# A new order table for every engine of a two-layer AdaLN kernel, all instructions unchanged

## What is computed

```python
mod = (_silu(L0_c) @ L0_wmod).reshape(L0_c.shape[0], 6, 1, -1)
h = _layernorm(x, axis=-1) * (1 + ca) + sa
x = x + ga * _L0_attn_ref(h, L0_attn_w_qkv, L0_attn_w_out)
h = _layernorm(x, axis=-1) * (1 + cb) + sb
x = x + gb * _L0_ffn_ref(h, L0_ffn_gate_kernel, ...)
...
h = _layernorm(x, axis=-1) * (1 + ca) + sa
x = x + ga * _L1_attn_ref(h, ...)
h = _layernorm(x, axis=-1) * (1 + cb) + sb
x = x + gb * _L1_ffn_ref(h, ...)
```

## Time and profile before

| | us |
|---|---|
| median of 3 runs | 1070.87 |
| the runs | 1074.27, 1070.87, 1070.3 |
| span of the profiled execution | 1072.8 |
| TensorE busy | 916.9 (85%) |
| VectorE busy | 773.2 (72%) |
| ScalarE busy | 656.1 (61%) |
| GpSimd busy | 428.5 (40%) |
| mean granted TensorE clock | 0.941 |

### The profile page before, as it was taken

How to read it: one execution, slowest core, us unless ns; L and a number is a source line. 1 busy time by engine, 2 the same in 40 slices (tenths; PEclk the granted TensorE clock), 3 DMA queues, 4 the chain that set the end, 5 groups by cost and what they waited for, 6 DMA issues and landing times. The chain is left out here.

```text
span 1072.8 us, 15618 instructions
## 1 busy us (share of the span) xinstructions
PE 916.9 (85%) x5176; PEld 507.8 (47%) x5176; DVE 773.2 (72%) x1467; ACT 656.1 (61%) x1176; POOL 428.5 (40%) x537
## 2 busy tenths in 40 slices
PE   4147778998899899999998899999998899879876
PEld 2111134443454355654444655455565365558744
DVE  6565678768866877788768686888878766447675
ACT  2235564666666768667667576776856756755442
POOL 3241042325131826554324265662545525265310
PEclk9557899999999999999999999999999899979978
DMA  8510214001300040115000014032010010010001
GB/s 233 163 55 30 63 39 101 31 2 56 60 1 2 14 118 9 40 31 126 4 1 14 22 45 99 31 90 41 18 35 19 3 38 2 9 41 7 18 10 35
DMA packets 54536, 47.09 MB, mean 44 GB/s; under 512 B 12393, under 2 KB 50025, under 8 KB 53114
## 3 DMA queue, kind: packets, MB, share of 16 engines
q1 hardware_dynamic: 53898, 45.85, 16.8%
q10 hardware_dynamic: 560, 0.26, 0.1%
HBM read 30.97 MB, written 14.73 MB: 43 GB/s over the span
## 5 line engine op out<-in xcount | busy, mean ns | idle before, releaser
L1565 DVE TENSOR_REDUCE negmax<-scores_for_max 128x2 f32<-128x1024 f32 x252 | 307.6, 1221 | 67.9 <-PE scores_for_max L940 66.0
L1277 ACT ACTIVATE probs<-scores 128x1024 f32<-128x1024 f32 x256 | 262.4, 1025 | 114.9 <-PE scores L964 112.2
L974 PE MATMUL weighted_values<-probs,vaug 128*32 128x512 f32 x1024 | 143.2, 634 | 3.6 <-ACT probs L1277 3.6
L1038 PEld LDWEIGHTS shared_ab<-eo,mu 128*128 128x128 f32 x1024 | 128.6, 191 | 35.6 <-issue 25.2
L1038 PE MATMUL shared_ab<-eo,mu 128*128 128x128 f32 x1024 | 141.1, 281 | 3.7 <-ACT scaled L1391 2.0
L1963 POOL TENSOR_TENSOR acc<-acc,scaled 128x512 f32<-128x512 f32 x55 | 71.7, 1304 | 169.6 <-ACT scaled L1391 169.6
L572 PE MATMUL expert_units<-hb_hi,e_lo 128*128 128x512 f32 x224 | 111.9, 500 | 16.7 <-DVE mu L1706 9.8
L940 PE MATMUL scores_for_max<-ks,qs 48*128 48x512 bf16 x504 | 102.1, 402 | 26.5 <-DVE negmax L1565 22.3
L1700 DVE SCALAR_TENSOR_TENSOR mu<-th,expert_units 128x512 f32<-128x512 f32 x112 | 76.7, 685 | 66.1 <-ACT th L1319 65.6
L964 PE MATMUL scores<-qs,ks 51*128 51x512 bf16 x512 | 102.2, 396 | 25.4 <-ACT probs L1277 23.7
L1319 ACT ACTIVATE th<-expert_units 128x512 f32<-128x512 f32 x112 | 66.9, 597 | 83.0 <-PE expert_units L574 81.8
(11 more groups left out here) (320 smaller groups left out, 1591.5 us busy)
## 6 DMA issues: line engine op xcount, KB each, us to landing
parts_d<-parts SPq DMA_DIRECT2D x15, 384.0 KB, 2.5
qs<-parts_d SPq DMA_DIRECT2D x14, 384.0 KB, 6.1
ks<-parts_d SPq DMA_DIRECT2D x14, 384.0 KB, 9.3
w<-in_L_ffn_w SPq DMA_DIRECT2D x16, 256.0 KB, 3.8
parts_d<-parts SPq DMA_DIRECT2D x15, 256.0 KB, 2.7
xp<-in_L_attn_x SPq DMA_DIRECT2D x8, 256.0 KB, 2.9
probs<-in_L_ffn_w_kernel SPq DMA_DIRECT2D x2, 1024.0 KB, 7.9
x<-in_L_attn_x SPq DMA_DIRECT2D x8, 256.0 KB, 2.9
```

What stands on the lines that cost most here:

```text
L974: last = nc.tensor.matmul(pv[32 * j:32 * j + 32, :], vaug[:, kt, PAIRS * (j // 2) + GP * g + j % 2, :], probs[:, kt % 2, j % 2, j // 2, :] ...
L1038: last = nc.tensor.matmul(m0[:, at], mu[:, (2 * e + f) % 4, at], eo[:, e, f, :], start=(f == 0), stop=(f == HALVES - 1))
L1277: nc.scalar.activation(probs[:, kt % 2, j, :, :].rearrange("p m s -> p (m s)"), se[:, :], ACT.Exp)\
L1565: V.tensor_reduce(negmax[:, g % 2, :, n], max_bank(b, g, n)[:, :].rearrange("p (m s) -> p m s", m=2), AX, ALU.max, negate=True)\
```

## The change

Only `SLOTS` differs. All 1344 TensorE, 872 ScalarE, 1032 VectorE, 272 GpSimd and 136 SyncE entries are there before and after; 1271, 816, 954, 252 and 123 of them stand at another place in their engine's order. The lines of the diff that name the steps of the text below, cut from the whole table:

```diff
@@ -67,237 +67,239 @@
 SLOTS = {
-    ("P", "load"): dict(sp=(1, 19, 28, 31, 48, 57, 79, 84)),
...
-    ("P", "xT"): dict(pe=(30, 60, 72, 178, 324, 531, 662, 880)),
...
-    ("P", "v"): dict(pe=(54, 62, 77, 199, 328, 645, 668, 1017), act=(14, 47, 106, 195, 274, 397, 465, 632)),
...
-    ("P", "stack"): dict(sp=(27, 40, 50, 61, 69, 83, 99, 108)),
...
-    ("C", "xT"): dict(pe=(465, 559, 807, 938, 1060, 1169, 1260, 1324)),
...
-    ("C", "out"): dict(pe=(538, 647, 885, 1012, 1117, 1227, 1307, 1335)),
...
-    ("C", "xT3"): dict(pe=(564, 768, 899, 1024, 1133, 1239, 1317, 1338)),
...
-    ("P", "e0hi"): dict(act=(20, 21, 24, 27, 38, 45, 46, 50)),
-    ("P", "e1hi"): dict(act=(49, 58, 59, 60, 85, 95, 100, 146)),
-    ("P", "whhi"): dict(act=(25, 28, 29, 33, 34, 43, 44, 102)),
...
-    ("P", "mod1"): dict(dve=(123, 194, 218, 222, 240, 244, 264, 298)),
...
-    ("P", "e0lo"): dict(dve=(176, 177, 180, 186, 193, 196, 197, 223)),
...
-    ("P", "raw"): dict(sp=(2, 3, 5, 11, 13, 16, 17, 18)),
...
+        ("P", "xT"): dict(pe=(54, 65, 69, 197, 327, 492, 644, 811)),
+        ("P", "v"): dict(pe=(62, 66, 172, 312, 471, 618, 778, 936), act=(51, 58, 110, 192, 289, 381, 482, 586)),
...
+        ("C", "xT"): dict(pe=(344, 512, 678, 854, 1003, 1134, 1260, 1324)),
...
+        ("C", "out"): dict(pe=(449, 638, 814, 976, 1097, 1205, 1302, 1337)),
+        ("C", "xT3"): dict(pe=(463, 657, 827, 994, 1104, 1219, 1312, 1338)),
...
+        ("P", "e0hi"): dict(act=(2, 15, 16, 17, 18, 19, 41, 42)),
+        ("P", "e1hi"): dict(act=(3, 43, 44, 45, 46, 47, 48, 49)),
...
+        ("P", "whhi"): dict(act=(6, 20, 21, 22, 23, 24, 27, 28)),
...
+        ("P", "e0lo"): dict(dve=(85, 86, 87, 88, 89, 90, 91, 92)),
...
+        ("P", "mod1"): dict(dve=(150, 157, 160, 161, 162, 163, 164, 165)),
...
+        ("P", "raw"): dict(sp=(1, 4, 5, 7, 8, 9, 10, 11)),
+        ("P", "load"): dict(sp=(2, 19, 34, 47, 55, 67, 79, 92)),
...
+        ("P", "stack"): dict(sp=(35, 39, 45, 54, 65, 78, 94, 104)),
```

More of the change, by code:

```diff
@@ L83 @@
[L83 to L88, removed]
@@ L160 @@
-    ("A", "wog"): dict(dve=(255, 339, 420, 534, 602, 731, 792, 924)),
-    ("B", "load"): dict(sp=(21, 55, 65, 77, 89, 103, 118, 128)),
-    ("B", "oT"): dict(pe=(169, 323, 477, 633, 786, 944, 1108, 1256)),
-    ("B", "ot"): dict(act=(109, 198, 283, 390, 480, 590, 693, 797)),
-    ("B", "y"): dict(pe=(170, 326, 479, 636, 793, 951, 1112, 1257)),
-    ("B", "x1"): dict(dve=(268, 356, 438, 540, 631, 733, 841, 936)),
-    ("B", "stats"): dict(dve=(269, 357, 440, 541, 633, 734, 842, 937)),
-    ("B", "rstd"): dict(pool=(37, 68, 89, 127, 152, 190, 217, 247)),
@@ L294 @@
-    ("P", "wT"): dict(pe=(26, 27, 28, 32, 33, 35, 39, 53)),
-    ("P", "wsplit"): dict(dve=(84, 85, 93, 101, 102, 104, 107, 110)),
-    ("P", "colm"): dict(pe=(31, 34, 36, 37, 42, 43, 44, 45, 46, 48, 49, 50, 51, 52, 57, 286)),
-    ("P", "cols"): dict(dve=(87, 112, 118, 119, 120, 121, 122, 191, 192, 199, 201, 202, 204, 211, 242, 281)),
-    ("P", "modpe"): dict(pe=(40, 47, 55, 56, 242, 335, 368, 414)),
-    ("P", "raw"): dict(sp=(2, 3, 5, 11, 13, 16, 17, 18)),
-    ("P", "late"): dict(sp=(4, 22, 23, 26, 32, 34, 35, 42)),
+        ("C", "out0"): dict(pe=(1, 2, 3, 4, 5, 6, 7, 1329)),
@@ new lines @@
+        ("C", "upb"): dict(pe=(8, 9, 10, 11, 12, 13, 14, 15, 16, 17, 18, 19, 20, 21, 1334, 1336)),
+        ("C", "row"): dict(pe=(22, 23, 24, 25, 26, 27, 28, 1254)),
+        ("P", "wT"): dict(pe=(29, 30, 31, 32, 33, 34, 35, 36)),
+        ("P", "colm"): dict(pe=(37, 38, 39, 40, 41, 42, 43, 44, 45, 46, 47, 48, 49, 50, 51, 52)),
+        ("P", "modpe"): dict(pe=(53, 55, 56, 57, 58, 59, 60, 61)),
+        ("P", "xT"): dict(pe=(54, 65, 69, 197, 327, 492, 644, 811)),
+        ("P", "v"): dict(pe=(62, 66, 172, 312, 471, 618, 778, 936), act=(51, 58, 110, 192, 289, 381, 482, 586)),
@@ new lines @@
+        ("P", "proj"): dict(pe=(63, 64, 67, 68, 73, 85, 204, 219, 333, 364, 529, 556, 707, 763, 818, 839)),
+        ("A", "max"): dict(pe=(70, 71, 72, 74, 75, 76, 77, 78, 79, 81, 82, 83, 86, 90, 92, 95, 97, 101, 103, 105, 108,
[11 rows of a table added]
+        1214), dve=(221, 222, 223, 225, 226, 227, 228, 229, 230, 231, 232, 233, 235, 236, 237, 238, 239, 240, 241,
[11 rows of a table added]
+        ("A", "mT"): dict(pe=(80, 100, 120, 142, 167, 194, 236, 265, 317, 337, 373, 418, 461, 491, 521, 555, 627, 647,
+        674, 715, 774, 808, 838, 877, 922, 965, 999, 1036, 1105, 1133, 1182, 1224)),
@@ new lines @@
+        ("P", "silu"): dict(act=(4, 5, 25, 26, 29, 30, 31, 32, 33, 34, 35, 36, 37, 38, 39, 40), dve=(102, 103, 112,
+        113, 114, 115, 116, 117, 118, 119, 120, 121, 122, 123, 124, 125)),
+        ("P", "whhi"): dict(act=(6, 20, 21, 22, 23, 24, 27, 28)),
+        ("P", "small"): dict(act=(7, 8, 9, 10, 11, 12, 13, 14)),
+        ("P", "hT"): dict(act=(50, 57, 62, 126, 200, 304, 397, 504)),
+        ("P", "split"): dict(act=(52, 55, 59, 63, 67, 77, 135, 144, 210, 230, 337, 351, 443, 481, 517, 534), dve=(167,
@@ new lines @@
+        ("P", "stats"): dict(dve=(93, 168, 219, 275, 349, 442, 536, 639)),
+        ("P", "wsplit"): dict(dve=(94, 95, 96, 97, 98, 99, 100, 101)),
+        ("P", "whlo"): dict(dve=(104, 105, 106, 107, 108, 109, 110, 111)),
+        ("P", "cols"): dict(dve=(126, 127, 136, 137, 138, 139, 140, 141, 142, 143, 144, 145, 146, 147, 148, 149)),
+        ("P", "mod1"): dict(dve=(150, 157, 160, 161, 162, 163, 164, 165)),
+        ("P", "lo"): dict(dve=(151, 152, 153, 154, 155, 156, 158, 159), pool=(2, 20, 26, 45, 68, 102, 134, 163)),
@@ new lines @@
+        ("P", "rot"): dict(dve=(166, 171, 218, 220, 224, 234, 293, 300, 359, 378, 484, 495, 588, 619, 657, 673)),
+        ("A", "wog"): dict(dve=(170, 274, 357, 453, 553, 655, 754, 848)),
+        ("P", "split3"): dict(dve=(172, 203, 204, 205, 206, 207, 208, 209, 210, 211, 212, 213, 214, 215, 216, 217),
+        pool=(8, 9, 24, 29, 32, 36, 48, 53, 76, 81, 111, 115, 144, 156, 172, 178)),
+        ("A", "onorm"): dict(dve=(243, 253, 261, 269, 291, 311, 329, 344, 372, 395, 415, 435, 465, 482, 503, 525, 556,
@@ new lines @@
+        ("C", "rstd3"): dict(pool=(89, 130, 165, 197, 215, 235, 262, 272)),
+        ("P", "raw"): dict(sp=(1, 4, 5, 7, 8, 9, 10, 11)),
+        ("P", "load"): dict(sp=(2, 19, 34, 47, 55, 67, 79, 92)),
+        ("P", "late"): dict(sp=(3, 6, 12, 13, 14, 15, 16, 17)),
+        ("P", "modst"): dict(sp=(18, 20, 21, 22, 23, 24, 25, 26)),
+        ("B", "load"): dict(sp=(27, 57, 68, 82, 95, 109, 119, 128)),
+        ("A", "load"): dict(sp=(28, 48, 58, 69, 84, 98, 111, 120)),
+        ("C", "loadd"): dict(sp=(29, 76, 89, 105, 115, 123, 130, 134)),
```

208 lines of the change are left out of this document (99 added, 109 removed), and 176 rows, old and new, of the table SLOTS.

## The result

The changed kernel takes 1123.49 us (median of 4 runs, 1117.45 to 1125.03), the kernel before 1070.59 (1069.92 to 1074.27) beside it: ratio 1.0468, 95% interval 1.0429 to 1.0508. It is slower, on the side forecast, but far outside the range: 53 us instead of 17. The profiled execution's span is 1121.2 us, 48.4 more than before's.

What follows compares the result with a forecast made beforehand. TensorE was taken as the bound from 148.2 to 940 us, with a serial chain before 77.04. Terms 12 + 2 + 4 - 1 = +17 us gave 1089.8 against the profiled span, a predicted median of 1088, range 1066 to 1105.

Steps and rivals of the forecast that it cites:

- The start: Batch 0's chain up to its first exp: first exp at 88.9, 11.9 us late, taken as +12, between 8 and 17.
- The sum: Step durations added along the start's chain, from the last raw load at 21.1 to the first exp at 88.9 us.
- The tail: The 133 us after the last exp: reordered up, keep and dn steps were to give -1 us, between -5 and +5.
- The count of cover: TensorE work between handoffs compared with the other engine's need: missing cover 105.2 us in the old table, 109.6 in the new.
- The two loops and the experts: Attention loops and expert handoffs: half of the +4.4 us in missing cover, taken as +2, between -10 and +8.
- C's first chain: From a batch's last down to its C.xT: too little TensorE work between, so stalls; +4 us, between 0 and 15.
- The clock: Gaps in TensorE's matmul stream halve its clock, so a stall may cost more than its length; C's term would be 8.
- Rival 3: Much slower: C's first chain late in each of batches 0 to 6 and costing clock, 15 + 8 more: 1108 us; chance 0.12.
- What would show it: Signs: e0hi at 21, hp_lo near 45, first maximum near 71, first scores 9 to 15 us late, rest 0 to 10 longer.

Runs made afterwards that it cites:

- splits_late: after with only the weight splits (e0hi, e1hi, whhi, small, e0lo, whlo, e1lo) put back where before has them; 1115.54 us, ratio 1.0390.
- first50_before: after with every step that had ended 48.5 us into before's trace in before's order, except e1hi, e0lo, e1lo; 1111.51 us, ratio 1.0334.
- tail_two: w0_ahead with two of batch 6's up steps and the transposition before them moved up to or behind batch 7's last down; 1127.03 us, ratio 1.0524.
- after: The changed kernel itself, against the kernel before; 1123.49 us, ratio 1.0468.
- stack_behind_row: after with SyncE's stack loads of batches 2, 4 and 7 put behind the first row of batches 1, 3 and 6; 1108.48 us, ratio 1.0331.
- after_again: The same order as after, measured once more; 1124.61 us, ratio 1.0529.
- w0_ahead: after with VectorE's products of batch 7's first two w0 moved ahead of its routing weights; 1123.82 us, ratio 1.0511.
- loads_ahead: three_back with some input and gate-row loads ahead of stack loads on SyncE, and the VectorE steps awaiting them two maxima further back; 1090.55 us, ratio 1.0179.
- three_back: after with first50_before, stack_behind_row and before's order from the end of batch 7's y together; 1089.04 us, ratio 1.0136.

## Why the prediction was wrong

- *The start, +12 (8 to 17).* The mechanism was right, the size a little low. The first `scores` is 17.3 us late and `y` of batch 0 21.1; splits_late and first50_before took 8.0 and 12.0 us off the median, 9.4 and 10.0 in the traces. The first `scores` came at 94.4 instead of 88.9. The sum gave `stats` and its follow-up 1.7 us and left out the last step, which took 2.39 us in before's trace and stood in the upper bound alone; it took 3.08 here. The first maximum was 4 us later than forecast (75.14), and the way from there to `scores` took 19.2 instead of 18.0, with three maxima ahead of batch 2's projection, not the two of the sum. "`mod1` stands ahead of `lo`" was counted in the chain and cost little by itself (0.9 us between splits_late and first50_before).
- *The missing term: SyncE's queue behind the start.* This is the step that failed most plainly, a cost put at nothing. The sum follows SyncE up to the first row and no further. `stack` of batches 2, 4 and 7 stands ahead of the first row of batches 1, 3 and 6 (for 7 with two small steps between) and goes out just when the row is wanted: 12.1 us of waits, 15 us of time, forecast as 0. Both orders were there to be read. By itself it doesn't make up the miss of 36 us; the tail (11 to 14 us off) and the loops (up to 17 off) do the rest.
- *The tail, -1 (-5 to +5).* Wrong in sign: 10 to 13 us. I counted "two of batch 6's `up` steps before the last `down`" as a gain. It is a loss, because the chain behind the last `down` is 53 us in both and everything ahead of it adds; but before has one of the two there as well, and most of the 10 us is waits. The count of cover did show it, 8.3 us missing in batch 7 before and 15.6 after, and the sum set this off against batches 1 to 6.
- *The two loops and the experts, +2 (-10 to +8).* Too small: with the other causes removed 14 to 19 us remain, some of them the start's. Waits for maxima rose from 22.3 to 37.0 us, as the cover said; those for exponentials fell from 23.7 to 14.6. The experts' waits for `mu`, for which the cover promised 7.7 us less, fell by 1.4 in batches 0 to 6 (15.6 to 14.2), and 6.4 came in batch 7, which is the tail. Cover counted in work says which handoffs are tight, not what they cost; which of them make up the rest stays open.
- *C's first chain, +4 (0 to 15).* It cost next to nothing. The transpositions of batches 0 and 5, for which a wait of some us was forecast, in the timeline:

```profile
299.20 0.66 PE L899 MATMUL shared_pc<-ident,xcn 128*128 128x128 f32 x4
...
887.10 0.66 PE L899 MATMUL shared_pc<-ident,xcn 128*128 128x128 f32 x4 [0.38 <-ACT xcn L1259]
```

  TensorE reached them 32.0 and 27.5 us after the last `down` (267.2 and 859.6), not after the 18.6 and 17.6 of work counted in between: time also passes in its waits and at half clock, and the chain uses it.
- *The clock.* "A stall may cost more than its length" held, and it was taken into no sum: 9.1 us for the wait of 5.60, with the clock at half for 23.9 us from 165.2 us on, 1.4 before its end. The Trainium skill's "TensorE: Matmul & The Clock Gate", section "HAM oscillation", warns of just that, and here the trace agrees.
- *Rivals.* Rival 3 (1108, stalls spread and cost clock) came nearest, but its place, C's chain, was wrong. The range ended at 1105 since no case joined a late start, a loose tail and row waits.
- *What would show it.* `e0hi` at 20.86 was right, `hp_lo` at 47.17 2 us late, the first maximum 4 us late and the first `scores` 2.3 us outside its 9 to 15; the rest of the span was to grow by 0 to 10 us and grew by 31 (1026.8 against 995.8).

## What to carry to other kernels

In a queue executed in order, look at each small transfer that someone waits for and at the large ones issued just ahead of it: here it lost 0 to 3.5 us to its turn and the rest on the way among their data. Find the last serial chain first; what is put ahead of its start is paid in full, and work behind its start is free only where it doesn't stand ahead of the chain's own steps (53 us, but 58.6 in tail_two). Losses read from a cover count are too rough to sum, and terms of opposite sign from different stretches shouldn't be set off against each other. A short wait in a matmul stream can cost more than its length (9.1 us for 5.6).

## What the hardware showed

- Three 6 KB rows issued behind 1.5 MB of stack data were waited for until 9.8, 7.3 and 8.6 us after their issue (after); issued ahead of them they held nobody up, and `exp` ran 5.4, 4.1 and 5.6 us after the issue (stack_behind_row).
- The same TensorE steps between `y` of batches 3 and 4 took 112.5 to 117.7 us in four traces (after, after_again, w0_ahead, tail_two) with no step changed before them, at a granted clock of 1.00 to 0.92. One profile can't carry a difference of 5 us.
- Removing waits doesn't always gain: loads_ahead had 8.8 us less idle time than three_back and 14.3 us more busy time, at a mean clock of 0.903 against 0.920.
